# Eight list tiles of the second experts, made sure by two of four batches, are fetched and worked on first

## The reference, cut to what matters

```
x = x + _L1_xattn_ref(_layernorm(x), ctx_1024, ...)
# then, with h = _layernorm(x), T = 2048 rows, E = 8 experts, I = 256
routes = h @ Wr                                   # T x 8
top_vals, top_idx = top_k(routes, 2)              # two experts a row
w = softmax(top_vals), put at top_idx             # T x 8
expert_out = (silu(h @ Wg[e]) * (h @ Wu[e])) @ Wd[e]
x = x + sum over e of w[t, e] * expert_out[t, e]
```

## Time and profile before

| | |
|---|---|
| median of three executions | 875.5 us |
| profiled execution | 874.6 us |
| its span, first to last instruction | 872.9 us |
| PE busy | 771.5 us, 88% |
| DVE busy | 459.6 us, 53% |
| POOL busy | 381.6 us, 44% |
| ACT busy | 373.0 us, 43% |
| mean granted TensorE clock | 0.948 of full |
| list fetches of the second experts (`XG<-lists_d`) | 39 of 65 KB, 1.8 us from issue to landing |
| result scatters of the second experts | 39, 957 ns each on GpSimd |

### The profile page before, as it was taken

One profiled execution on the slowest core, in us unless ns is written; L12 is line 12 of the kernel. 1 busy time (PEld: TensorE's weight loads), 2 busy tenths in 40 slices (PEclk: granted clock), 3 DMA queues, 4 the chain that ended last, 5 costly groups with the idle time before them and its releaser, 6 DMA issues. The chain is left out here.

```text
span 872.9 us, 13958 instructions
## 1 busy us (share of the span) xinstructions
PE 771.5 (88%) x4682; PEld 448.1 (51%) x4682; DVE 459.6 (53%) x1030; ACT 373.0 (43%) x562; POOL 381.6 (44%) x369
## 2 busy tenths in 40 slices
PE   5899999999999999999999999879995586339990
PEld 4655556455566455556455455465664343315550
DVE  4635364465464665554564565344442488526662
ACT  4464554454554464554454453112332444204440
POOL 6435443644543563634464534332322306735551
PEclk9999999999999999999999999989999599559996
DMA  9999999300000000000020003001111500112225
GB/s 221 152 151 150 150 151 144 108 1 1 2 1 1 10 5 1 1 2 1 7 103 1 2 1 97 13 12 39 44 40 53 162 2 29 47 49 68 74 62 157
DMA packets 76795, 50.45 MB, mean 58 GB/s; under 512 B 4052, under 2 KB 72536, under 8 KB 76728
## 3 DMA queue, kind: packets, MB, share of 16 engines
q1 hardware_dynamic: 73208, 42.30, 28.8%
q0 software_dynamic: 3520, 7.27, 2.5%
HBM read 20.07 MB, written 29.47 MB: 57 GB/s over the span
## 5 line engine op out<-in xcount | busy, mean ns | idle before, releaser
L733 ACT ACTIVATE PT<-PSUM 128x1024 f32<-128x1024 f32 x128 | 127.9, 1025 | 164.9 <-PE PSUM L1365 164.0
L600 POOL TENSOR_TENSOR PSUMS<-PSUMS,PT 128x1024 f32<-128x1024 f32 x64 | 152.2, 2379 | 101.9 <-ACT PT L733 97.1
L1007 DVE TENSOR_REDUCE TOPS<-PSUM 128x2 f32<-128x1024 f32 x128 | 151.5, 1221 | 53.5 <-PE PSUM L1329 53.5
L600 POOL TENSOR_TENSOR PSUMS<-PT 128x1024 f32<-128x1024 f32 x32 | 76.4, 2386 | 162.0 <-ACT PT L733 161.8
L1383 PE MATMUL PSUM<-PT,BIG 128*64 128x512 f32 x512 | 130.8, 611 | 0.8 <-ACT OT L746 0.8
L1501 PE MATMUL PSUM<-BIG,XGT 128*128 x170 | 84.6, 602 | 0.0
L997 DVE TENSOR_TENSOR QL<-PSUM,QH 128x512 fp32r<-128x512 f32 x32 | 22.1, 691 | 97.2 <-ACT QH L713 97.2
L1138 DVE TENSOR_TENSOR SIL<-SIL,PSUM 128x256 f32<-128x256 f32 (+1 forms) x62 | 32.2, 520 | 63.9 <-ACT SIL L783 63.9
L1365 PE MATMUL PSUM<-TOPROW,MINUS 64*128 64x512 f32 x320 | 63.4, 392 | 0.6 <-ACT TOPROW L718 0.6
L783 ACT ACTIVATE SIL<-PSUM 128x256 f32<-128x256 f32 (+1 forms) x62 | 28.7, 463 | 80.9 <-PE PSUM L1501 80.9
L739 ACT ACTIVATE PTC<-PSUM 32x1024 f32<-32x1024 f32 x32 | 32.5, 1014 | 62.1 <-PE PSUM L1365 62.1
(11 more groups left out here) (242 smaller groups left out, 1414.2 us busy)
## 6 DMA issues: line engine op xcount, KB each, us to landing
lists_d<-EMPTY SPq DMA_DIRECT2D x3, 2730.0 KB, 47.8
lists_b<-EMPTY SPq DMA_DIRECT2D x3, 2470.0 KB, 44.3
BIG<-in_L_ffn_w SPq DMA_DIRECT2D x2, 2048.0 KB, 9.1
lists_d<-EMPTY SPq DMA_DIRECT2D x1, 2665.0 KB, 45.4
XG<-lists_d SPq DMA_DIRECT2D x39, 65.0 KB, 1.8
lists_b<-EMPTY SPq DMA_DIRECT2D x1, 2405.0 KB, 19.4
W2ALL<-in_L_ffn_w SPq DMA_DIRECT2D x4, 512.0 KB, 6.1
PT<-results_d SPq DMA_DIRECT2D x8, 256.0 KB, 5.0
```

The lines of the kernel that those rows point to most:

```text
L600: pool.tensor_tensor(PSUMS[:, i % 2], PTT[:, i % 2, 0] if kt == 1 else PSUMS[:, i % 2], PTT[:, i % 2, kt], ALU.add).then_inc(s_ps, 1)
L733: act.activation(PTT[:, i % 2, kt], PSUM[:, place:place + 2, :], ACT.Exp, scale=DH ** -0.5).then_inc(s_exp, 1)
L1007: dve.tensor_reduce(TOPS[:, c, 0, :], PSUM[:, place:place + 2, :], AX.X, ALU.max).then_inc(s_max, 1)
```

## The change

Two batches put 2 x 2 x 512 = 2048 pairs into eight parts. At most 127 rows of each part can be outside full tiles, so at least (2048 - 8 x 127) / 128, rounded up to 9, tiles are full once batches 0 and 1 are sent; the change takes 8 of them (`EARLY[1]`). It makes tables for these eight from the counts after two batches (`EARLY_TABLES`), in a new step `e_tables3` of the hand-written order, on VectorE between the slots of batch 2 and the logits of batch 3. SyncE fetches these eight first, waiting only for the early tables and for batches 0 and 1. The final tables, now for the other 31 tiles, start behind the tiles done (`DONE`, `NEXT`, `LINB`); they are made on VectorE inside the loop of the second experts, ahead of `gated(1)`. The number of list tiles stays 39. The stage of the first experts keeps its tables and their place.

```diff
+    KNOWN = [B, 2]
+    EARLY = [0, -(-(2 * KNOWN[1] * S - E * (P - 1)) // P) - 1]
...
-            "r_turn2 r_front1 r_logits2 r_hot2 r_back1 r_rest2 c_proj3 r_stats3 r_run2 r_scale3 r_norm3 r_slot2 "
+            "r_turn2 r_front1 r_logits2 r_hot2 r_back1 r_rest2 c_proj3 r_stats3 r_run2 r_scale3 r_norm3 r_slot2 e_tables3 "
...
     # SyncE
-                sp.wait_ge(*TABLES.at(which, "row_of"))
-                for b in (B - 2, B - 1):
-                    sp.wait_ge(*rows_done(which, b))
+                if EARLY[which]:
+                    sp.wait_ge(*EARLY_TABLES.at(0, "row_of"))
+                    for b in (KNOWN[which] - 2, KNOWN[which] - 1):
+                        sp.wait_ge(*rows_done(which, b))
                 for j in range(n_tiles):
+                    if j == EARLY[which]:
+                        sp.wait_ge(*TABLES.at(which, "row_of"))
+                        for b in (B - 2, B - 1):
+                            sp.wait_ge(*rows_done(which, b))
...
     # GpSimd, constants
+                pool.memset(NEXT[:, E - 1:E], float(N)).then_inc(CONST.sem, 1)
...
     # VectorE
-            def tables(which):
+            def tables(which, early):
+                steps, run = (EARLY_TABLES, 0) if early else (TABLES, which)
+                rest = not early and EARLY[which] > 0
+                first, n = (0, EARLY[which]) if early else (EARLY[which], n_tiles - EARLY[which])
...
+                elif early:
+                    dve.wait_ge(s_dn, TILES_B)
+                    dve.wait_ge(*RD1[KNOWN[which] - 1].at(0, "run3"))
                 else:
-                    dve.wait_ge(s_dn, TILES_B)
+                    dve.wait_ge(*EARLY_TABLES.at(0, "base"))
                     dve.wait_ge(*RD1[B - 1].at(0, "run3"))
+                if early:
+                    tell(dve.scalar_tensor_tensor(out=has, in0=RUN[0:1, which, KNOWN[which] * TPB, :]...,
+                                                  scalar=float(1 - P), in1=lin, op0=ALU.add, op1=ALU.is_gt))
...
+                if early:
+                    tell(dve.tensor_scalar(DONE[0:1, :], incl, float(n * P), None, ALU.min))
+                    after("done")
+                    dve.wait_ge(*CONST.at(0, "next"))
+                    tell(dve.scalar_tensor_tensor(out=NEXT[0:1, 0:E - 1], in0=DONE[0:1, 1:E], scalar=float(N),
+                                                  in1=DONE[0:1, 0:E - 1], op0=ALU.add, op1=ALU.subtract))
+                    tell(dve.tensor_scalar(LINB[0:1, 0:n_tiles - n], LIN[0:1, 0:n_tiles - n], DONE[0:1, 0:1], None, ALU.add))
...
                 for j in range(n_tiles + 2):
+                    if which == 1 and j == 1:
+                        tables(which, False)
                     if j < n_tiles:
                         gated(j)
...
+                elif name == "e_tables":
+                    tables(1, True)
+                    dump_rows(1)
             experts(1)
...
     # TensorE, turn_x
+                    if j == 0 and EARLY[which]:
+                        pe.wait_ge(*EARLY_TABLES.at(0, "w_of"))
+                    if j == EARLY[which]:
+                        pe.wait_ge(*TABLES.at(which, "w_of"))
                     if j == 0:
-                        pe.wait_ge(*TABLES.at(which, "w_of"))
                         read_columns(0)
```

More of the change, by code:

```diff
@@ L136, in build @@
         ROW_OF = sb("ROW_OF", TILES_D, dt=I32)
+        DONE = sb("DONE", E)
+        NEXT = sb("NEXT", E)
+        LINB = sb("LINB", TILES_D)
         W_OF = sb("W_OF", TILES_D, dt=I32)
@@ L219, in build @@
                                       "minus1", "minus2", "rows1", "rows", "rows_c0", "rows_c1", "rows_c", "iota0", "iota1",
-                                      "spread1", "spread", "tie", "lower", "incl0", "incl", "run"])
+                                      "spread1", "spread", "tie", "lower", "incl0", "incl", "run", "next"])
         s_lin = sem("lin")
@@ L277, in build @@
                                        "exp", "w_of"])
+        EARLY_TABLES = Steps(sem("early_tables"), ["has", "used", "mul", "shift", "incl", "incl2", "passed", "moved", "row",
+                                                   "row_of", "exp", "w_of", "done", "next", "base"])
         s_dump = sem("dump_rows")
@@ L1066, in tables @@
                 r, c = LINROW[0:1, 0, 0:n], LINROW[0:1, 1, 0:n]
+                lin = LIN[0:1, :].rearrange("p (e t) -> p e t", e=E)
                 def after(name):
-                    dve.wait_ge(*TABLES.at(which, name))
+                    dve.wait_ge(*steps.at(run, name))
                 def tell(i):
-                    i.then_inc(TABLES.sem, 1)
+                    i.then_inc(steps.sem, 1)
                 dve.wait_ge(s_lin, 1)
@@ L1079, in tables @@
                     dve.wait_ge(*RD0.at(B - 1, "run3"))
+                elif early:
+                    dve.wait_ge(s_dn, TILES_B)
+                    dve.wait_ge(*RD1[KNOWN[which] - 1].at(0, "run3"))
                 else:
-                    dve.wait_ge(s_dn, TILES_B)
+                    dve.wait_ge(*EARLY_TABLES.at(0, "base"))
                     dve.wait_ge(*RD1[B - 1].at(0, "run3"))
-                tell(dve.tensor_tensor(has, RUN[0:1, which, NT, :].unsqueeze(2).broadcast_to([1, E, NT]),
-                                       LIN[0:1, :].rearrange("p (e t) -> p e t", e=E), ALU.is_gt))
+                if early:
+                    tell(dve.scalar_tensor_tensor(out=has, in0=RUN[0:1, which, KNOWN[which] * TPB, :].unsqueeze(2).broadcast_to([1, E, NT]),
+                                                  scalar=float(1 - P), in1=lin, op0=ALU.add, op1=ALU.is_gt))
+                else:
+                    tell(dve.tensor_tensor(has, RUN[0:1, which, NT, :].unsqueeze(2).broadcast_to([1, E, NT]), lin, ALU.is_gt))
                 after("has")
@@ L1089, in tables @@
                 tell(dve.tensor_tensor(TAB8[0:1, :, :], INCL[0:1, :, :], used.unsqueeze(1).broadcast_to([1, E, E]), ALU.mult))
-                tell(dve.tensor_scalar(shift, used, float(-P), float(N), ALU.mult, ALU.add))
+                if rest:
+                    tell(dve.scalar_tensor_tensor(out=shift, in0=used, scalar=float(-P), in1=NEXT[0:1, :], op0=ALU.mult, op1=ALU.add))
+                else:
+                    tell(dve.tensor_scalar(shift, used, float(-P), float(N), ALU.mult, ALU.add))
                 after("mul")
@@ L1093, in tables @@
                 after("incl")
-                tell(dve.tensor_scalar(incl, incl, float(P), None, ALU.mult))
+                if rest:
+                    tell(dve.scalar_tensor_tensor(out=incl, in0=incl, scalar=float(P), in1=DONE[0:1, :], op0=ALU.mult, op1=ALU.subtract))
+                else:
+                    tell(dve.tensor_scalar(incl, incl, float(P), None, ALU.mult))
                 after("incl2")
@@ L1102, in tables, with dump_rows @@
                 after("row")
-                tell(dve.tensor_tensor(ROW_OF[0:1, 0:n], r, LIN[0:1, 0:n], ALU.add))
+                tell(dve.tensor_tensor(ROW_OF[0:1, first:first + n], r, LINB[0:1, 0:n] if rest else LIN[0:1, 0:n], ALU.add))
                 tell(dve.tensor_reduce(c, pa, AX.X, ALU.add))
                 after("exp")
-                tell(dve.tensor_scalar(W_OF[0:1, 0:n], c, float(E - 1), float(BANK), ALU.min, ALU.mult))
-            def experts(which):
+                tell(dve.tensor_scalar(W_OF[0:1, first:first + n], c, float(E - 1), float(BANK), ALU.min, ALU.mult))
+                if early:
+                    tell(dve.tensor_scalar(DONE[0:1, :], incl, float(n * P), None, ALU.min))
+                    after("done")
+                    dve.wait_ge(*CONST.at(0, "next"))
+                    tell(dve.scalar_tensor_tensor(out=NEXT[0:1, 0:E - 1], in0=DONE[0:1, 1:E], scalar=float(N), in1=DONE[0:1, 0:E - 1],
+                                                  op0=ALU.add, op1=ALU.subtract))
+                    tell(dve.tensor_scalar(LINB[0:1, 0:n_tiles - n], LIN[0:1, 0:n_tiles - n], DONE[0:1, 0:1], None, ALU.add))
+            def dump_rows(which):
                 FF, n_tiles, before, SETS = stage(which)
-                tables(which)
                 if which == 1:
@@ L1113, in experts @@
                 dve.tensor_scalar(DUMP[:, 0:n_tiles], JP[:, 0:n_tiles], float((which + 1) * N + 1), None, ALU.add).then_inc(s_dump, 1)
+            def experts(which):
+                FF, n_tiles, before, SETS = stage(which)
+                if which == 0:
+                    tables(which, False)
+                    dump_rows(which)
                 def keep_x(j):
```

1 line of the change is left out of this document (removed).

## The result

The changed kernel takes 871.64 us, the median of 20 executions (862.56 to 874.78), against 876.25 of 20 of the kernel before: ratio 0.9932, interval 0.9912 to 0.9951. It is faster by 4.6 us and not by 12.6: clear of the noise, yet only 0.7%, and the time lies above the range given. Two of the 20 executions, of 862.56 and 862.58 us, lie inside it. The profiled execution has 871.1 us, its span 869.4.

The account below looks back on a forecast made before the run. Bound by GpSimd's sends (17.17 us of TensorE idle), then TensorE on 39 tiles. Gain 15.48 - 2.86 = 12.62 us: span 872.9 - 12.6 = 860.3, plus 1.7 and 0.9, rounded to 863.0 us; range 861.3 to 866.5.

Parts of the forecast that it names:

- transpose of tile 4: TensorE's first work on list tile 4, at 770.72 instead of 783.34, after 2.86 us of new stall.
- tile 8 fetched: SyncE's fetch of the first tile not made early, at 775.05 behind the last send, landing at 776.90.
- transpose of tile 8: TensorE's first work on list tile 8, near 778.1, 1.2 us after its rows land, waiting for nothing.
- Early tables: New VectorE tables after batch 2's slots: 3.3 us within 6.31 us of idle time, so no cost.
- Early fetch: SyncE's eight fetches beside batch 2's sends: first at 753.3, eighth 8.12 us later, all in SBUF by 763.3.
- The final tables in the loop: VectorE's tables for 31 tiles before gated(1): 3.32 us, stalling TensorE 2.86 us before tile 4.
- Start of tile 0: TensorE's first list-tile transpose at 762.10 instead of 777.58, 15.48 us earlier.
- The clock: TensorE's rise from 0.50 holds through the new stall: cost taken as 0, against 1.9 us if it falls.
- rival A: TensorE's clock falls in the new stall, costing 1.9 us: 864.9 us, chance 0.17.
- The prediction's own sign of being wrong: The clock showing 0.5 after 771 would mean the prediction is wrong; it expected 1.00 from about 768.
- B: VectorE's stretch is shorter than counted, so TensorE waits for tile 8: gain at most 13.8, 861.7 us, chance 0.06.
- C: VectorE's tile work stretches GpSimd's batch 3 sends, delaying tile 8's fetch: gain 9.7, 865.8 us, chance 0.10.

Follow-up runs that it names:

- same_after: The changed kernel, unaltered, run again side by side with two variants: 860.89 us, ratio 0.9852 against the kernel before (873.0 us).
- early3: The changed kernel with three list tiles made early instead of eight: 873.92 us, ratio 0.9961 against the kernel before.
- early5: The changed kernel with five list tiles made early instead of eight: 866.67 us (ratio 0.9928), and 868.32 us (0.991) in the fourth set.
- fourth set: Changed kernel, tables_first, early5 and a variant with final tables in five parts, beside the kernel before (876.83 us): 870.0, 866.0, 868.32 and 869.56 us.
- hold: The changed kernel with the eight early tiles fetched only once all sends have landed: 879.74 us, ratio 1.0041 against the kernel before.
- tables_first: The changed kernel with the final tables straight behind batch 3's slots, ahead of the first tile's copy on VectorE: 862.86, 862.25 and 866.0 us in three sets.
- loads32: tables_first with SyncE reading 32 register values in place of the early fetches, the eight fetches coming behind the last send: 880.24 us, one execution.
- second and third set: Runs beside the kernel before at 874.03 and 873.0 us: four variants at 861.71 to 872.25 us, then same_after and two variants at 860.59 to 862.25.
- first, fourth and fifth: Sets of runs beside the kernel before at 876.12, 876.83 and 875.86 us; the changed kernel took 869.18, 870.0 and 870.46 us in them.
- act_fetch: The changed kernel with the eight early fetches issued by ScalarE's queue instead of SyncE's: 869.87 us, ratio 0.9918 against the kernel before.
- loads_only: tables_first with SyncE only reading twelve table entries into a register early, and fetching behind the sends: 872.25 us, one execution.

## Why the prediction was wrong

The direction was right, and same_after shows the working itself to be right within half a microsecond at every step where nothing is stretched. Point by point, forecast, then the profiled execution of the result, then same_after:

| step | forecast | result | same_after |
|---|---|---|---|
| early fetches, first to eighth start | 753.3 to 761.4 | 754.96 to 774.46 | 753.74 to 761.88 |
| transpose of tile 0 | 762.10 | 764.05 | 762.44 |
| final tables | 3.32 us | 7.99 us | 3.33 us |
| transpose of tile 4 | 770.72 | 777.49 | 771.16 |
| last send | 771.91 | 773.89 | 772.04 |
| tile 8 fetched | 775.05 | 780.13 | 775.15 |
| transpose of tile 8 | 778.12 | 787.27 | 778.35 |
| span | 860.3 | 869.4 | 860.5 |

*Early tables.* 751.82 to 755.03, in VectorE's idle time; nothing was lost there.

*Early fetch: this step failed.* It took three issues from the earlier trace rows, made when GpSimd was not sending, for the pace of eight beside its sends. That was 19.5 us in place of 8.1. By itself this cost nothing: each tile still came before it was wanted. "They run beside batch 2's sends" was said of the transfers and never asked of the instructions. The one trace the prediction had could not warn of it: by the mark given below under the start of tile 0, it is a trace in which nothing is stretched.

*The final tables in the loop: the term of the sum that was mis-sized.* 3.32 us against 7.99. The mechanism (VectorE holds bank 7, TensorE waits at tile 4) was right, and the wait carries the full 4.7 us more. Three profiled executions of the sets that were stretched have short tables in the same place of the loop: 3.48 us in early3 and 3.57 in early5 (fourth set), where SyncE has no fetch beside them, and 3.31 in hold, where the sends are gone. With the sends and SyncE in its slow steps, but no tile's work beyond the first transpose, they were 3.80 us (tables_first, fourth set) and 4.03 (loads32). The 7.11 to 7.99 us were seen in the four profiled executions of the stretched sets that had all three together. That all three are needed is read from these single executions; it is not tested by itself.

*Start of tile 0.* 1.95 us later than forecast in the profiled execution. Batch 3's `PLACE` was already 763.11 - 761.23 = 1.88 late, and batch 1's first send 740.83 - 739.03 = 1.80, 14 us ahead of the first early fetch. ScalarE's rows show a stretch there, in code that the change leaves alone; the kernel before stands first, the changed one below:

```profile
727.30 0.60 ACT L816 ACTIVATE OT<-PSUM 128x512 f32<-128x512 f32 x1 [2.38 <-PE PSUM L1235]
...
731.07 1.94 ACT L810 ACTIVATE PT<-PSUM 128x1024 f32<-128x1024 f32 x2 [2.17 <-PE PSUM L1580]
```

```profile
727.29 0.60 ACT L832 ACTIVATE OT<-PSUM 128x512 f32<-128x512 f32 x1 [4.00 <-remote]
...
734.57 1.94 ACT L826 ACTIVATE PT<-PSUM 128x1024 f32<-128x1024 f32 x2 [3.83 <-PE PSUM L1633]
```

From the one to the other are 3.77 us before and 7.28 after. Batch 0's sends run beside it (722.89 to 732.8), and SyncE issued nothing between 680.5 and 754.96. This interval is a mark of the occasion. It is 3.76 to 3.77 us in the kernel before and in all seven traces of the second and third set, and 5.36 to 8.11 us in the result and in all eleven traces of the first, fourth and fifth. So what stretches instructions on some occasions is there ahead of any early fetch, and the start of tile 0 belongs to it. The medians of the kernel before fit: 875.9 to 876.8 us in the stretched sets, 873.0 and 874.0 in the others.

*The clock.* 0 was taken, rival A said 1.9; in the result it was 2.38. It fell in a stall of 6.86 us, and held in one of 2.44 in same_after. The prediction's own sign of being wrong, 0.50 after 771, is there from 774 on. So the 0 was right for the stall forecast, and A is a consequence of the longer one. From the rule of the Trainium skill named there (TensorE: Matmul & The Clock Gate, "What's actually happening"), that activity releases the throttled clock, the prediction read a cost of 1.9 us. The fall in the longer stall is in line with that reading; same_after, with 1.00 through its stall of 2.44 us, is not.

Against the forecast, tile 8 is 787.27 - 778.12 = 9.15 us late: 1.95 at tile 0, 2.38 from the clock, and the rest, 4.82, on the way to tile 4, of which the tables are 4.67.

*Rivals B and C.* Neither came. In the result batch 3's sends took 0.95 to 0.96 us beside the first tiles' work on VectorE, the last one 1.14; in same_after all took 0.95 to 0.96. The rule of the Trainium skill that C names (SBUF — State Buffer, "Who interferes with whom") would have shown as longer sends, and beyond that one of 1.14 us no run here shows them. What suffered was the other engines' instructions.

*What stays open.* Why it comes on some occasions. In three sets and the result itself the changed kernel was stretched (869.2 to 871.6 us, kernel before 875.9 to 876.8), in one it was not (860.9, before 873.0), nor were its kin in another (before 874.0). The first and the third set ran on the same chip, so it isn't the chip alone, and the two executions of 862.6 us in the result, of which there is no trace, suggest that it differs within a set too. Two rivals stand untested. Every execution on record has a span and a granted clock, so none is known to have run unobserved, and a part of the profiler in the stretch isn't ruled out. And the slow instructions come two or three together every 0.7 us, many of them shorter than usual (a register read of 5 ns where 267 is the median). That fits instructions that reach the sequencer late as well as instructions that are held up in it; no run tells the two apart. How the stretch reaches VectorE's waits is not shown either. The Trainium skill (Perfetto Trace Analysis, "DMA Instruction — HWDGE (DVE, Sync)") says that the DVE and Sync sequencers share the block that makes hardware descriptors. loads32 speaks against that as the cause: SyncE was stretched without issuing a DMA. act_fetch does not bear on it, as its tables came after ScalarE's fetches.

**A version that may be safer.** tables_first is 862.3 us where the changed kernel is 860.9 (third set, intervals overlap), and 866.0 where that is 870.0 (fourth set, 0.9886 against 0.9932 of before; the intervals, 0.9863 to 0.9908 and 0.9908 to 0.9957, just touch, with four executions each). Its tables were spared in the fourth set, 3.80 us, and the stall of 3.65 us falls at tile 1, ahead of the clock's rise. Of the versions that ran it is the likeliest choice; that it is the better one rests on those four executions.

## What to carry to other kernels

A transfer that is moved into a busy stretch brings its instructions along: count them (here six a fetch), look up what the sequencers of the other engines do at that time, and take their pace from a row where both ran, or keep a bound well above it. A serial chain of small dependent instructions goes where the least work waits behind it; on stretched occasions TensorE waited 6.86 us for it at tile 4, and 3.65 at tile 1. When a result differs from its forecast, compare first a stretch of code that the change does not touch: here it showed on every trace, ahead of the change, which kind of occasion it was. And run the changed kernel again in every set: the second set left it out, and only same_after showed that its times do not speak for the order of the tables.

## What was not expected of the hardware

On some occasions, while GpSimd issues indirect DMAs at 1.26 us each, the instructions of another sequencer come in steps of about 0.7 us after its first twenty or so: 19.5 us for the eight fetches that take 8.1 otherwise, 24.4 for 32 register reads that would take 18 at the 0.56 of loads_only, an estimate. It follows the work from SyncE to ScalarE. VectorE's waits for its own last instruction grow by 0.3 to 2.0 us each, and its table of twelve instructions from 3.3 to 8.0 us. SyncE need not be at work for it: from ScalarE's copy of `OT` to its copy of `PT`, beside batch 0's sends, are 7.28 us in place of 3.77. GpSimd's own sends keep 0.95 to 0.96 us. The same text of kernel gave 860.9 and 869.2 us on one chip within the hour.
